# Retention and mixture of experts on one core: the order inside a part is changed, and x comes by channels from part four on

## The reference

```python
def _L0_attn_ref(x, W_q, W_k, W_v, W_o, gn_weight, gn_bias):
    q = (x @ W_q.T).reshape(b, t, h, dh)          # k and v alike
    attn = jnp.einsum('bihd,bjhd->bhij', q, k) * decay[None] / scale
    y = jnp.einsum('bhij,bjhd->bihd', attn, v)
    mean = y.mean(axis=(1, 3), keepdims=True)
    var = y.var(axis=(1, 3), keepdims=True)
    yn = (y - mean) / jnp.sqrt(var + EPS)
    yn = yn.reshape(b, t, dm) * gn_weight + gn_bias
    return yn @ W_o.T
def _L0_ffn_ref(x, t_emb, sw1, sb1, sw3, sb3, sw2, sb2, w1, b1, w2, b2):
    shared = jax.nn.silu(xf @ sw1 + sb1) * (xf @ sw3 + sb3) @ sw2 + sb2
    for k in range(TOPK):
        exp_ids = (tok * PRIME + k * HASH_OFF) % E
        ...
        h = jax.nn.gelu(jnp.einsum('enc,ech->enh', xs, w1) + b1[:, None, :], approximate=False)
        y = jnp.einsum('enh,ehc->enc', h, w2) + b2[:, None, :]
        out = out.at[sort_idx].add(y.reshape(N, C))
    out = out / TOPK
    return ((shared + out) / (N_SHARED + 1)).reshape(B, T, C)
x = x + _L0_attn_ref(_layernorm(x, axis=-1), ...)
x = x + _L0_ffn_ref(_layernorm(x, axis=-1), ...)
```

## Time and profile before

| | us |
|---|---|
| median of 3 runs | 434.4 (433.68 to 434.84) |
| the profiled execution | 434.14, of which its span is 432.3 |
| busy: PE, DVE, ACT, POOL | 426.3, 339.4, 210.4, 74.9 |
| granted TensorE clock, mean | 1.000 (2.4 GHz) |

### The profile page before, as it was taken

One profiled execution on the slowest core, in us unless ns is written; L12 is line 12 of the kernel. 1 busy time (PEld: TensorE's weight loads), 2 busy tenths in 40 slices (PEclk: granted clock), 3 DMA queues, 4 the chain that ended last, 5 costly groups with the idle time before them and its releaser, 6 DMA issues.

```text
span 432.3 us, 14448 instructions
## 1 busy us (share of the span) xinstructions
PE 426.3 (99%) x6276; PEld 385.8 (89%) x6276; DVE 339.4 (79%) x803; ACT 210.4 (49%) x403; POOL 74.9 (17%) x69
## 2 busy tenths in 40 slices
PE   7999999999999999999999999999999999999997
PEld 6899999999999999998989988899888999888996
DVE  6888899877987889977798887978879878746423
ACT  3555556445744467445247325473344834346530
POOL 2103323522353122550510000100001000000000
PEclk9999999999999999999999999999999999999999
DMA  8533332232331131225420016000142001120011
GB/s 273 181 112 102 100 102 76 77 110 75 120 98 52 52 117 55 89 94 192 164 84 2 0 50 227 17 0 1 49 155 88 0 1 49 49 97 2 0 50 49
DMA packets 15816, 34.66 MB, mean 80 GB/s; under 512 B 2416, under 2 KB 3088, under 8 KB 15248
## 3 DMA queue, kind: packets, MB, share of 16 engines
q1 hardware_dynamic: 15328, 33.18, 22.6%
q10 hardware_dynamic: 432, 0.66, 0.5%
HBM read 25.44 MB, written 8.40 MB: 78 GB/s over the span
## 4 chain that ended last, share of the span: by engine, by line
PE 98%; DVE 1%; ACT 1%; issue 0%; ACTq 0%
PE bank L379 54%; PE bank L388 13%; PE bank L389 7%; PE bank L457 7%; PE bank L500 4%; PE bank L487 4%; PE bank L471 3%; PE bank L436 2%; PE bank L397 1%; PE bank L647 1%; PE bank L518 1%; PE bank L581 0%; ACT kexp L703 0%; PE bank L512 0%; DVE vexp L1171 0%; DVE xlo L1187 0%
## 5 line engine op out<-in xcount | busy, mean ns | idle before, releaser
L379 PE MATMUL bank<-x2hi,sw_hi 128*128 128x512 f32 x128 | 51.3, 400 | 0.0
L379 PE MATMUL bank<-x2lo,sw_hi 128*128 128x512 f32 x128 | 50.4, 394 | 0.0
L379 PE MATMUL bank<-x2hi,sw_lo 128*128 128x512 f32 x128 | 50.3, 393 | 0.0
L718 ACT ACTIVATE keo<-kT,msk 128x512 f32<-128x512 f32 x32 | 21.4, 715 | 49.4 <-DVE kT L900 49.4
L388 PE MATMUL bank<-w_both,ehi 128*128 128x512 f32 x124 | 44.9, 397 | 0.0
L388 PE MATMUL bank<-sw_both,ghi 128*128 128x512 f32 x124 | 44.8, 394 | 0.0
L911 DVE TENSOR_TENSOR pm<-bank,msk 128x512 f32<-128x512 f32 x64 | 39.8, 682 | 6.4 <-PE bank L457 6.1
L788 ACT ACTIVATE sil<-bank,s1b 128x512 f32<-128x512 f32 x32 | 22.0, 688 | 46.6 <-PE bank L379 46.6
L1076 DVE STREAM_TRANSPOSE x2t<-xl 32x256 f32<-32x256 f32 x96 | 41.8, 436 | 1.7
L379 PE MATMUL bank<-xhi,wqkv_hi 128*128 128x256 f32 x128 | 38.2, 298 | 1.3 <-DVE xlo L895 0.7
L807 ACT ACTIVATE ehi<-xres 128x512 fp32r<-128x512 f32 x32 | 20.2, 633 | 32.9 <-PE bank L389 32.4
(11 more groups left out here) (139 smaller groups left out, 1111.8 us busy)
## 6 DMA issues: line engine op xcount, KB each, us to landing
w_raw<-w SPq DMA_DIRECT2D x16, 256.0 KB, 3.1
xres<-xs SPq DMA_DIRECT2D x16, 256.0 KB, 3.4
x_scratch<-xres SPq DMA_DIRECT2D x16, 256.0 KB, 2.8
xl<-x_scratch SPq DMA_DIRECT2D x8, 512.0 KB, 4.3
xr<-x_scratch SPq DMA_DIRECT2D x4, 1024.0 KB, 4.8
xin<-xa SPq DMA_DIRECT2D x15, 256.0 KB, 2.9
out<-xr SPq DMA_DIRECT2D x7, 512.0 KB, 2.6
sw_raw<-sw SPq DMA_DIRECT2D x6, 256.0 KB, 3.9
```

The costliest lines, as they stand in the source:

```text
L379: mm = nc.tensor.matmul(o, w[c][l], x[c][r], start=first and c == 0 and j == 0, stop=last and c == n - 1 and j == 2)
L718: cp = nc.scalar.activation(keo[:, :, :, odd, :], kT[:].rearrange("p g (c j) -> p c g j", c=CPS), ACT.Copy, scale=parity[:, odd:odd + 1])
```

## The change

From part 3 on (`TURNED`, the fourth part) PE no longer transposes x: the host hands x over a second time, by channels (`xt`), and SP loads it into `xin_t`. The factor of the layer norm is then needed along the row. DVE turns POOL's factors with four 32 x 32 transposes (`turn_rstd`), SP stores them to DRAM in two packets and reads them back for all partitions (`load_rstd`), and DVE multiplies (`scale_x`) and splits (`split_x`). The mean is not subtracted: each column's mean is taken out of the weights instead. PE multiplies the weights by -1/256 once (`weight_means`), POOL adds the result to them (`centre_w`), and ACT and POOL split them anew during steps 0 and 1 (`high_centred`, `low_centred`), to be used from part 3 on. In all parts the order of a step changes: PE projects k and q first, then the state sums, and `from_state` comes after `project_v`; DVE decays before it adds the state, and makes xhi and xlo before the low half of y. ACT copies k by tokens before it copies y. The bias of the slots is loaded at the end of the retention instead of in steps 10 and 14, ahead of the last store of x1, and added one gate later in the first batch. There are four warm-up matmuls instead of six.

```diff
+                if NSUP <= h < NSUP + TURNED:
                     sp.wait_ge(t_done, h - NSUP + 2)
+                elif h >= NSUP + TURNED:
+                    sp.wait_ge(ln_stats, h - NSUP + 1)
                 sp.dma_start(xin[h % NSUP][:], xa[h]).then_inc(x_landed[h % NSUP], 16)
+
+            def load_xt(h):
+                if h >= TURNED + 2:
+                    sp.wait_ge(xlo_ready, h)
+                sp.dma_start(xin_t[h % 2][:], xt[h]).then_inc(xt_landed[h % 2], 16)
+
+            def store_rstd(h):
+                sp.wait_ge(rstd_turned, h - TURNED + 1)
+                sp.dma_start(rstd_dram[h].rearrange("(t n) -> t n", t=TILES), ln_turned[0:TILES, :]).then_inc(rstd_stored, 16)
+
+            def load_rstd(h):
+                sp.wait_ge(rstd_stored, (h - TURNED + 1) * 16)
+                if h >= TURNED + 2:
+                    sp.wait_ge(x_scaled, h - TURNED - 1)
+                sp.dma_start(rstd_row[h % 2][:], rstd_dram[h].partition_broadcast(P)).then_inc(rstd_landed, 16)
...
                 if h in LOAD_STEPS:
                     load_ffn(2 + LOAD_STEPS.index(h), 0)
-                sp.wait_ge(s_done, h + 1)
+                if TURNED <= h + 2 < PARTS:
+                    load_rstd(h + 2)
+                if h + 1 < PARTS:
+                    sp.wait_ge(q_done, h + 2)
+                else:
+                    sp.wait_ge(s_done, h + 1)
...
+                if h + 1 < PARTS:
+                    sp.wait_ge(v_done, h + 2)
+                if h + 6 < PARTS:
+                    load_x(h + 6)
+                if h == 11:
+                    sp.wait_ge(ln_stats, PARTS - 2)
+                    load_xl(0, 0)
+                if h == 13:
+                    sp.wait_ge(ln_stats, PARTS)
+                    load_xl(0, 1)
+                if h + 3 < PARTS:
+                    store_rstd(h + 3)
...
+            for j in range(3):
+                store_x1(last, j)
+
+            sp.wait_ge(bias_stored, 16)
+            sp.wait_ge(o_done, NBATCH * 4)
+            sp.wait_ge(xres_biased, NBATCH * 4)
             for j in range(4):
-                store_x1(last, j)
+                load_slot_bias(j)
+            store_x1(last, 3)
             for j in range(4):
                 sp.wait_ge(x1_stored[j], NBATCH * 16)
...
+            def weight_means(n, o):
+
+                pe.wait_ge(mean_set, 2)
+                w = [x[:, n, c, :] for c in range(CB) for x in (wqkv_hi, wqkv_lo)]
+                for j, x in enumerate(w):
+                    mm = nc.tensor.matmul(o, minus_mean[:], x, start=j == 0, stop=j == len(w) - 1)
+                mm.then_inc(wmean_done, 1)
+
...
-                if h == 0:
-                    project_k(1)
-                state_sums(h)
-                if 0 < h < PARTS - 1:
-                    project_k(h + 1)
-                if b and s == 0:
-                    pe.wait_ge(pm_ready, h * PAIRS + 1)
-                    head_means(b - 1, p_bank[0])
-                if h + 1 < PARTS:
-                    project_q(h + 1)
-                else:
-
+                if h + 1 == PARTS:
+
+                    state_sums(h)
                     transpose_x2(0)
                     pe.wait_ge(pm_ready, h * PAIRS + 1)
                     output(b - 1, 2, p_bank[2])
-                if h + 1 < PARTS:
-                    from_scores(h, True)
-                    from_state(h, False)
-                else:
                     from_state(h, True)
                     transpose_x2(1)
                     pe.wait_ge(pm_ready, h * PAIRS + 2)
...
                         pe.wait_ge(pm_ready, h * PAIRS + (j + 1))
                         transpose_x2(j)
                     from_scores(h, False)
+                    return
+
+
+                project_k(h + 1)
+                if b and s == 0:
+                    pe.wait_ge(pm_ready, h * PAIRS + 1)
+                    head_means(b - 1, p_bank[0])
+                project_q(h + 1)
+                state_sums(h)
+                from_scores(h, True)
+                if b and s == 1:
+                    output_bias(b - 1, p_bank[1])
+                if b and s >= 2:
+                    for j in range(2 * (s - 2), 2 * (s - 2) + 2):
+                        output(b - 1, j, p_bank[j])
+                k_by_tokens(h + 1)
+                if h + 2 < TURNED:
+                    transpose_x(h + 2)
                 if b and s == 0:
                     head_vars(b - 1, p_bank[0])
-                if b and s == 1:
-                    pe.wait_ge(pm_ready, h * PAIRS + 2)
-                    output_bias(b - 1, p_bank[1])
-                if b and s >= 2 and h + 1 < PARTS:
-                    for j in range(2 * (s - 2), 2 * (s - 2) + 2):
-                        pe.wait_ge(pm_ready, h * PAIRS + (j + 1))
-                        output(b - 1, j, p_bank[j])
-                if h + 1 < PARTS:
-                    k_by_tokens(h + 1)
-                    project_v(h + 1)
-                    if h + 2 < PARTS:
-                        transpose_x(h + 2)
-                    scores(h + 1)
+                project_v(h + 1)
+                from_state(h, False)
+                scores(h + 1)
...
-            warm_up(WARM_UP[1])
+            pe.wait_ge(wlo_ready, 1)
+            weight_means(1, p_bank[0][:, 0:D])
             project_k(0)
             project_q(0)
             project_v(0)
             k_by_tokens(0)
             transpose_x(1)
+            pe.wait_ge(wmean_copied, 1)
             scores(0)
+            weight_means(0, y_bank[:, 0:D])
+            weight_means(2, y_bank[:, D:2 * D])
...
+            def high_centred(i):
+
+                act.wait_ge(w_centred, i + 1)
+                act.wait_ge((k_done, q_done, v_done)[i], TURNED)
+                n = (1, 0, 2)[i]
+                nc.scalar.activation(wqkv_hi[:, n], wqkv_raw[:, n], ACT.Copy).then_inc(wchi_ready, 1)
...
+                if h == TURNED - 2:
+                    high_centred(0)
+                    high_centred(1)
                 if h + 1 < PARTS:
                     spread_k(h + 1)
                 else:
                     for j in range(4):
                         high_x2(0, j)
-                high_y(h)
                 if b and s == 1:
                     copy_bias(b - 1, p_bank[1])
                 if h + 1 < PARTS:
                     copy_k(h + 1)
+                if h == TURNED - 2:
+                    high_centred(2)
+                high_y(h)
+                if h + 1 < PARTS:
                     copy_v(h + 1)
...
+            def turn_rstd(h):
+                dve.wait_ge(ln_rstd, h + 1)
+                if h > TURNED:
+                    dve.wait_ge(rstd_stored, (h - TURNED) * 16)
+                for q in range(4):
+                    tr = nc.vector.transpose(ln_turned[0:32, 32 * q:32 * q + 32], ln_r[32 * q:32 * q + 32, :])
+                tr.then_inc(rstd_turned, 1)
+
+            def scale_x(h):
+
+                x = xin_t[h % 2]
+                dve.wait_ge(xt_landed[h % 2], (h - TURNED + 2) // 2 * 16)
+                dve.wait_ge(rstd_landed, (h - TURNED + 1) * 16)
+                nc.vector.tensor_tensor(x[:], x[:], rstd_row[h % 2][:].unsqueeze(1).broadcast_to([P, CB, SUPER]), ALU.mult).then_inc(x_scaled, 1)
+
+            def split_x(h):
+
+                dve.wait_ge(x_scaled, h - TURNED + 1)
+                dve.wait_ge(v_done, h)
+                nc.vector.tensor_copy(xhi[:], xin_t[h % 2][:]).then_inc(xhi_ready, 1)
+                dve.wait_ge(xhi_ready, h + 2)
+                nc.vector.tensor_tensor(xlo[:], xin_t[h % 2][:], xhi[:].bitcast(F32), ALU.subtract).then_inc(xlo_ready, 1)
...
                     mask_scores(h, range(PAIRS))
+                    decay_k(h + 1)
+                    decay_q(h + 1)
                     add_state(h)
                     if b and s == 0:
                         gn_spread(b - 1, p_bank[0])
-                    decay_k(h + 1)
-                    decay_q(h + 1)
                     carry_state(h)
...
-                low_y(h)
-                y_sums(h)
+                if TURNED <= h + 2 < PARTS:
+                    scale_x(h + 2)
                 if h + 3 < PARTS:
-                    ln_apply(h + 3)
+                    turn_rstd(h + 3)
                 if b and s >= 2:
                     for j in range(2 * (s - 2), 2 * (s - 2) + 2):
                         residual(b - 1, j, p_bank[j])
                 if h + 3 >= PARTS:
                     ln2_apply(0, h + 3 - PARTS)
-                if h + 2 < PARTS:
+                if b and s == 0:
+                    gn_eps(b - 1, p_bank[0])
+                if h + 2 < TURNED:
                     high_x(h + 2)
                     low_x(h + 2)
+                elif h + 2 < PARTS:
+                    split_x(h + 2)
+                low_y(h)
+                y_sums(h)
...
+                if i - (b == 0) in BIAS_GATES:
+                    n = BIAS_GATES.index(i - (b == 0))
...
+            def centre_w(i):
+
```

(8 more changed lines are left out.)

120 lines of the change are left out of this document (77 added, 43 removed).

## The result

The changed kernel takes 435.92 us (median, 434.81 to 437.14), the kernel before 434.25 us beside it (433.68 to 435.13). The ratio is 1.0042, with a 95% interval of 1.0031 to 1.0053: slower by 0.4%, where 430.0 us, 1% faster, was forecast. The profiled execution is the fastest of the seven (434.81 us), with a span of 433.0 us against 432.3. All seven had a mean granted clock of 0.991 to 0.996.

What follows compares the result with a forecast made beforehand. TensorE, busy 99% of the span, was taken as the bound: 434.14 - 5.85 (transposes) + 0.4 (start) + 0.9 (VectorE's lateness) + 0.35 (v's copy) = 429.9 us, 430.0 against the median; range 428.0 to 432.8.

Steps and rivals of the forecast that it cites:

- the timetable of VectorE: VectorE's cycle 9.96 us against TensorE's 9.91, a tie; masks 0.4 to 0.5 us late in plain steps; +0.9 us in all.
- TensorE's list: TensorE, parts 3 to 15: four transposes of x go, 0.45 us a part, 13 times, -5.85 us; seams taken as 0.
- rival D: xhi from SBUF is quick, no step stalls, the start costs nothing: 428.6 us, or 428 with faster seams; chance 0.10.
- Rival C: TensorE's seams take what the transposes gave, 0.3 a step: 433.9 us, no change to be told; chance 0.06.
- Waits only at steps 5, 9 and 13, 0.9 us in all: TensorE waits on masks or xlo only there, 0.3 us for each of the three batches after the first.
- The four small transposes: On VectorE, the 32 x 32 transposes of the factors, taken at 0.1 us each, 0.4 in all.
- rival A: VectorE becomes the bound because small transposes cost what large ones do, 1.74 us for 0.4: 441 us; chance 0.08.
- The power of 1.07 beside the scaling: GpSimd's power takes 1.07 us, normally 0.70, beside scale_x in every step; transposes begin 1.35 us after the variance.
- The copy of x: VectorE's xhi, from SBUF at twice the PSUM rate, might cost some 0.3 us less; the forecast did not count it.
- The wait on `vexp`: ScalarE copies y ahead of v; in the last part the state sums come first and wait: +0.35 us once.
- Rival B: The factor's way through DRAM is too long, scale_x about half a microsecond late, step 10.3 us: 433 us; chance 0.07.
- SP's extra load is issued a whole step ahead: SP's extra load of 256 KB a part, issued a whole step ahead of scale_x, costed at nothing.

Runs made afterwards that it cites:

- 431.88: Changed kernel with small transposes behind x's split, spread right behind scaling, second layer norm's first apply one part later, v copied before y once: 431.88 us, 0.9933.
- 427.82: Kernel of 431.88 us without scale_x, turn_rstd and the factor's store and load, x only centred from part 3 on: 427.82 us, 0.9839.
- the unturned one: Kernel of 431.88 us with the factors not turned, SP storing them straight from their column in 256 packets of 4 bytes: 507.16 us, 1.1517.

## Why the prediction was wrong

The step that failed is the timetable of VectorE, which gave 0.9 us of waits. In its place the runs show two losses. The places where TensorE waits on VectorE or ScalarE, with the lower clock behind one of them, are worth 4.0 us (435.92 to 431.88). What came with the factor's way is worth another 4.1 (431.88 to 427.82). The forecast had 1.25 us for all of it.

**TensorE's list: right.** The parts gain 0.57 us each where nothing is late (forecast 0.45), and with VectorE relieved the kernel comes to 427.8, beside rival D's 428 to 428.6. Rival C, dearer seams, is refuted: they were 0.12 cheaper. The order of blocks mattered, though, as the state sums between k and q showed, and I took 0 for it. The start cost 0.2 us in place of 0.4 (the second part's scores begin at 24.84, before at 24.62), with 0.5 us of idle time without a releaser in it. Something that I had at nothing was gained: the feed-forward phase, from its first matmul on, takes 234.8 us in place of 235.5, in all kernels with the changed order; why is open. And 429.9 for an execution 0.26 under the median is 430.2, not 430.0; that slip changes nothing.

**"Waits only at steps 5, 9 and 13, 0.9 us in all": wrong.** The timetable let VectorE's masks start 0.4 to 0.5 us late in a plain step; in the third part they were 1.3 late. That "all lateness is gone" at s = 2 and 3 failed in step 14, where s is 2. Two steps of VectorE's timetable were left out. At h = 13 the second layer norm's apply stands ahead of x's split, where the plain step has nothing of the kind; in the order of before k was taken only after the state sums, and it had time. The wait is 1.36 us, and the clock at its lower level adds 1.5 in the profiled execution; I had no term for the clock. Shown by moving that step alone: 2.9 us by the medians, and a mean clock below 0.999 in one run of six, where the changed kernel has it in seven of seven. And `scores` at s = 1 waits for the spread of the group norm, which the change had moved behind the transposes: three waits, 2.5 us in its profile. I had costed the spread's length and not who waits for it. By itself it isn't worth its 2.5 us: moved early, the lateness came out elsewhere.

**The four small transposes: mis-sized.** 0.84 us, not 0.4; 0.21 each is just under the 0.23 from which rival A was to decide. VectorE's cycle was indeed longer than TensorE's in the plain parts, and yet rival A by itself isn't what happened: 0.6 us a part taken off it gave nothing that can be measured. Moved late together with the other two steps, the transposes cost TensorE nothing that its waits show.

**The power of 1.07 beside the scaling: right**, 1.08 to 1.10 in all but two of these parts in place of 0.70, and the trace agrees with the Trainium skill ("SBUF — State Buffer", the section on the two separate sides). The same showed in a place that I hadn't thought of: 3.32 us instead of 1.38 for the apply beside GpSimd's bias. **The copy of x: mis-sized** to the other side, 0.43 us from SBUF instead of 0.69 from PSUM; the trace agrees with the Trainium skill ("VectorE: DVE Perf Modes", the perf-mode tier table) in kind, though the gain is 1.6 times and not twice. **The wait on `vexp`: right**, 0.30 against 0.35. **Rival B: refuted**: the row of factors landed in 3.2 us and the scaling of the changed kernel waited for it nowhere.

**"SP's extra load is issued a whole step ahead", at nothing: wrong.** I asked only whether the transfer is in time, not whom it delays. On the kernel before such transfers cost 1.9 us, with no computing engine waiting for them. That they do it through TensorE's instructions is likely and not shown to the end. For it stands that traffic alone raised the idle time without a releaser (0.6 to 2.1 us on one kernel, none to 0.9 on the other), and where that time ends: in the fourteen kernels besides the unturned one and that of before, all 32 such idle times of 0.25 us or more from 12 us on end 1.2 to 1.6 us behind a packet of TensorE's instruction queue. They also stand at fixed places of the list, one behind the same matmul of part 2 in ten of these kernels. Against a simple story stands that the packets aren't longer for it (1.09 us on the mean in the kernel before, 1.07 in the changed one, 1.10 with the traffic added to before), and that the order alone, without any added transfer, has 1.0 to 1.1 us of this idle time too, where before has none. So the new order has a part in it, and how a transfer holds up the instructions is open. The Trainium skill ("Runtime: NRT & Kernel Launch", Instruction fetch mechanics) says that an engine fetches its next 16 KiB of instructions over a DMA queue of its own while it runs, mostly hidden. The trace agrees with the size, 44 packets of 16 KB; wholly hidden the fetching was in the kernel before alone.

**The account.** Five of the kernels stand one above the other. 427.8 us is the new list with its late places mended, x by channels and nothing for the factor; 429.8 has the factor's read as traffic too; 431.9 has the scaling, the small transposes and the store; 433.0 has the spread, the transposes and v where the change has them; 435.9 is the changed kernel, with the apply there too. The steps are 2.0, 2.1, 1.2 and 2.9 us by the medians. The intervals of the first two kernels overlap, and so do those of the third and the fourth, so these two steps are the least sure. The lowest kernel is what was forecast without its waits: 430.0 - 0.9 - 0.35 = 428.7. Open stays what makes the 2.1 us between 429.8 and 431.88: the scaling and the transposes on VectorE, or the store of the factors. By the profiles, 1.7 us of it are more idle time without a releaser (3.8 against 2.1).

## What to carry to other kernels

When a step of the bottleneck engine is moved to the front of its part, look at every part for what stands ahead of its input on the other engines, above all in the first and last ones, where the list differs; a stall of 1.4 us cost 3 here, with the lower clock behind it. A transfer that is early enough isn't free: 384 KB in each of 13 parts, for which no computing engine waited, cost 1.9 us here, and stores in packets of 4 bytes cost 75. Look for idle time of the bottleneck engine that no semaphore ends, and whether it ends behind a packet of its instruction queue. And an operation of VectorE that is moved out of the way must not land beside a long one of GpSimd (3.32 us here for 1.38): look up what runs there first.

## What the runs showed of the hardware

- TensorE's instructions come in 44 packets of 16 KB, 0.9 to 2.1 us each in fifteen kernels, and up to 10.0 us in the one that stores 256 packets of 4 bytes a part; TensorE stood still for up to 7.1 us there.
- Idle time of TensorE that no semaphore ends (32 times of 0.25 us or more, in fourteen kernels) ended 1.2 to 1.6 us behind one of these packets each time.
- The four 32 x 32 transposes on VectorE take 0.21 us each, where 32 x 256 ones take 0.436: an eighth of the elements in half the time.
- Four instructions of 128 x 256 in SBUF took 3.32 us beside GpSimd's operation on 128 x 512, and 1.37 to 1.38 us elsewhere.
- After 1.36 us without work, which ended at 175.40, TensorE's granted clock was at 1.2 GHz for most of the time from 176 to 180 us. That isn't a matter of the wait's length alone: the idle 1.44 us at 42 us of the 431.88 us kernel and a wait of 1.8 us in the kernel with the transposes late alone had 1.00 behind them. With the unturned factors, where the idle time of 7.07 us ends at 37.99, it was 0.57 from 37 to 42 us.
